# Ternary weights prepared in pieces during the last attention batch, with their sign test and load on GpSimd, and the first feed-forward steps spread over the attention's tail

## The chip, the cores and the metric

One core of one Trainium2 chip runs the whole program. The metric is the device time of one execution in microseconds (us), taken as the median of several runs.

## What is computed

Two transformer layers on x of 4 batches of 512 tokens, 256 wide. The first layer (windowed attention, then a mixture of experts) is untouched by the change. The second is full attention with 16 heads of width 16, then a feed-forward part whose two weight matrices (1024 by 256, and 256 by 1024) are replaced by ternary ones:

```
scale = maximum(mean(abs(w)), 1e-8)
w_q   = clip(round(w / scale), -1, 1)       # in the kernel: (w > scale/2) - (w < -scale/2)
h = gelu(x @ w1_q.T + b1);  out = h @ w2_q.T + b2
```

So the ternary weights need three passes over each matrix: a sum of absolute values (then a sum over the partitions, by a matmul with ones), a test against -scale/2, and a step that makes the test against +scale/2 and subtracts.

## The kernel before

The parts run one after the other: attention 0 (A), experts (B), attention 1 (C), feed-forward (D). Within C and D each engine runs its own program, written out by hand and tied to the others by semaphores.

**Part C.** `pair_step(b, n, new, old, following)` handles pair n (two heads, n = 0 to 7) of batch b, in eight places i = 0 to 7. At each place TensorE makes one score tile (L1689) into one of three PSUM banks, and VectorE takes its negated row maximum (L1006), which frees the bank: TensorE can be at most three tiles ahead. Older pairs are worked on at the same places: the transposed scores (L1702), their Exp on ScalarE (L1341), the products with the values (L1728), and every second pair a transpose (L1742), a reciprocal (L1033) and a scaling (L1035), after which the next transpose of the maxima (L1714) may use its bank. Extra work hangs on fixed places: the layer norm of the next batch (statistics in pair 1, L659), the projections of the next batch, the transposes of the previous batch's output (L1640) and its output projection (L1647). `keep_raw` (L1327) copies bank 0 to a two-slot ring `raw`, and GpSimd takes it from there: low parts (L600) or the residual add (L610). After the last batch, four more steps (`TAIL1 = 4`, `pair_step(BATCHES, n, False, True, False)`) finish what is under way, with no new score tiles.

**Part D.** `mlp_step(b, f, ...)` for f = 0 to 8: TensorE makes hidden tile f (L1837, four matmuls), ScalarE applies Gelu (L1393) and copies a high part (L1398), VectorE subtracts to get the low part (L1098), and TensorE multiplies tile f-2 by the second matrix (L1814, eight matmuls). At f = 8 the next batch is transposed (L1428). The steps of batch 0 stand after tail steps: `MLP_AFTER = {2: (0,), 3: (1, 2, 3, 4, 5, 6, 7, 8)}`, that is all but one behind the tail's last step.

**The ternary weights.** SyncE loads both matrices and a bias in batch 0 of C (L469, 1 MB each). VectorE takes the absolute sum of each whole matrix (L1071, 128x2048 elements) after pairs 6 and 7 of batch 0. In the tail, after step 0, TensorE sums over the partitions (L1849), and VectorE makes the scales (L1044 to L1048), then for each matrix a whole test (L1054, into `wneg`) and a whole `scalar_tensor_tensor` (L1056). TensorE waits for both before hidden tile 0.

GpSimd's order in the last batch of C: two low parts, the reciprocal root of the layer norm (L493), the norm's application (L593), two low parts, two residual adds; then the tail's two residual adds, and for each batch of D the bias (L639), with the reciprocal root of the next norm ahead of it.

Of the kernel before, what the change touches and what calls it, by code (L numbers as in the profile page):

```python
# [21 lines left out]
P = 128  # L22
BATCHES, SEQ, D = 4, 512, 256
TT = SEQ // P
KT = D // P
# [48 lines left out]
QUANT_EPS = 1e-8  # L74


def build(nc, dram, out):
    with ExitStack() as ctx:
# [92 lines left out]
        wabs = sb("wabs", [P, 2], where=part_c)  # L171
# [10 lines left out]
        sb("gap_c1", [P, 56], where=part_c)  # L182
# [16 lines left out]
        wneg = sb("wneg", [P, KT * DFF], where=part_d)  # L199
# [23 lines left out]
        wd_loaded, b2_loaded = sem("wd_loaded"), sem("b2_loaded")  # L223
# [125 lines left out]
        def _(sp):  # L349
# [132 lines left out]
        def _(pool):  # L482
# [128 lines left out]

            for b in range(BATCHES):
# [5 lines left out]
                norm_apply(i, (b + 1) % BATCHES)  # L618
                if b + 1 < BATCHES:
# [12 lines left out]
            for half in range(2):  # L632
                add_out(BATCHES, half, half)
# [10 lines left out]
            for b in range(1, BATCHES):  # L644
# [5 lines left out]
        def _(dve):  # L650
# [390 lines left out]
            def ternary_scales():  # L1041

                dve.wait_ge(wabs_summed, 1)
                V.tensor_scalar(wscl[:], ps[:, 1, 0:2], 1.0 / (DFF * D), QUANT_EPS, ALU.mult, ALU.max  # L1044
                                ).then_inc(quant_step, 1)
                dve.wait_ge(quant_step, 4)
                V.tensor_scalar(whalf[:], wscl[:], 0.5, None, ALU.mult).then_inc(quant_step, 1)
                V.tensor_scalar(wmhalf[:], wscl[:], -0.5, None, ALU.mult).then_inc(quant_step, 1)  # L1048
                dve.wait_ge(quant_step, 6)

            def ternary_weights(i):

                wait(dve, quantized, i)
                V.tensor_scalar(wneg[:], flat[i], wmhalf[:, i:i + 1], None, ALU.is_lt).then_inc(quant_step, 1)  # L1054
                dve.wait_ge(quant_step, 7 + i)
                V.scalar_tensor_tensor(tern[i], flat[i], whalf[:, i:i + 1], wneg[:], ALU.is_gt, ALU.subtract  # L1056
                                       ).then_inc(quantized, 1)
# [7 lines left out]
            for n in range(1, PAIRS):  # L1065
                pair_step(0, n, True, False, True)
                if n >= PAIRS - 2:

                    i = n - (PAIRS - 2)
                    dve.wait_ge(wd_loaded, 3 * 16)  # L1070
                    V.tensor_reduce(wabs[:, i:i + 1], flat[i], AX.X, ALU.add, apply_absolute_value=True  # L1071
                                    ).then_inc(quant_step, 1)
# [30 lines left out]
            for n in range(TAIL1):  # L1103
                pair_step(BATCHES, n, False, True, False)
                if n == 0:
                    ternary_scales()
                    ternary_weights(0)
                if n == 1:
                    ternary_weights(1)
                for f in MLP_AFTER.get(n, ()):  # L1110
                    mlp_step(0, f, True, False, True)
# [10 lines left out]
        def _(act):  # L1122
# [206 lines left out]
            def pair_step(b, n, new, old, following):  # L1329
# [604 lines left out]
```

## Time and profile before

| | us |
|---|---|
| median of 3 runs | 1415.06 (1414.72 to 1417.81) |
| the profiled execution, its own time | 1412.89 |
| its span in the profile | 1411.2 |
| TensorE busy | 1350.9 (96%) |
| VectorE busy | 1057.3 (75%) |
| ScalarE busy | 729.5 (52%) |
| GpSimd busy | 477.8 (34%) |
| mean granted TensorE clock | 0.977 of full speed |

The busy times are sums over parts with different limits. A row of the profile names the engine, the line, the tiles and the mean duration; PE is TensorE, PEld its weight loads, DVE VectorE, ACT ScalarE, POOL GpSimd and SP SyncE. A line of the timeline gives start and duration in us, then in brackets the idle time before it and what ended it. Part C runs from about 1056 to 1317, its four batches some 65 us each, the tail to about 1344, and D to the end at 1411.

### The profile page before, as it was taken

The page shows a single profiled execution, that of the slowest core. Times are in us where ns is not written, and L with a number is a line of the kernel's source. Part 1 is how long each engine was busy: PE and PEld are TensorE (multiplying, and loading weights), DVE is VectorE, ACT ScalarE, POOL GpSimd, SP SyncE. Part 2 cuts the span into 40 slices and gives each one's busy share as a digit, 9 for nine tenths or more (in the row PEclk, how much of TensorE's full clock was granted, in tenths as well). Part 3 has the DMA queues.
Part 4 walks back from the last instruction along what each step waited for, and adds up shares of the span by engine and source line. Part 5 has one row for each costly group of instructions (what it writes and reads, how often), then busy time and mean ns, then how long its engine had stood idle before and what let it go on. Part 6 is the DMA issues. An engine that isn't in the chain of part 4 may idle for free.

```text
span 1411.2 us, 25588 instructions
## 1 busy us (share of the span) xinstructions
PE 1350.9 (96%) x8082; PEld 1075.3 (76%) x8082; DVE 1057.3 (75%) x2464; ACT 729.5 (52%) x1899; POOL 477.8 (34%) x728
## 2 busy tenths in 40 slices
PE   5799999999999999899999999999999999999898
PEld 3688988988898899788888888888884344444487
DVE  6889999989999999567655455444647887787475
ACT  4775565556555655454432232233325676767465
POOL 5766657765776576200000000000003131321031
PEclk9999999999999999999999999999996999999899
DMA  5200000000000000045311211103152333332001
GB/s 183 86 30 1 2 1 2 2 4 1 1 2 1 1 1 1 24 150 157 125 46 60 62 38 61 65 30 102 61 179 104 105 105 121 113 127 76 0 16 45
DMA packets 45892, 80.92 MB, mean 57 GB/s; under 512 B 5608, under 2 KB 13928, under 8 KB 45484
## 3 DMA queue, kind: packets, MB, share of 16 engines
q1 hardware_dynamic: 45484, 79.35, 17.2%
q8 instruction: 60, 0.98, 0.3%
q14 instruction: 60, 0.49, 0.1%
q0 software_dynamic: 288, 0.10, 0.1%
HBM read 64.70 MB, written 15.87 MB: 57 GB/s over the span
## 4 chain that ended last, share of the span: by engine, by line
PE 68%; DVE 13%; issue 5%; POOL 3%; ACT 2%; DVEq 0%; ACTq 0%; POOLq 0%
PE ps L1419 14%; PE ps L1421 13%; PE ps L1420 13%; PE ps L1689 5%; PE ps L1728 5%; PE ps L1506 3%; PE ps L1462 3%; PE ps L1814 2%; DVE ssum L805 2%; DVE qkn L794 2%; PE ps L1837 2%; DVE yT L769 1%; PE ps L1714 1%; PE ps L1702 1%; DVE nmax L785 1%
## 5 line engine op out<-in xcount | busy, mean ns | idle before, releaser
L1006 DVE TENSOR_REDUCE nm<-ps 128x1 f32<-128x512 f32 x256 | 166.1, 684 | 51.8 <-PE ps L1689 51.5
L1341 ACT ACTIVATE pT<-ps 128x512 f32<-128x512 f32 x256 | 143.5, 598 | 65.2 <-PE ps L1702 63.2
L493 POOL TENSOR_TENSOR ln_rs<-ln_ve,minus_half 128x4 f32<-128x4 f32 x12 | 15.1, 1262 | 434.0 <-DVE ln_ve L666 434.0
L1419 PE MATMUL ps<-xnT_lo,w1moe_hi 128*128 128x512 f32 x400 | 160.2, 401 | 0.0
L1420 PE MATMUL ps<-xnT_hi,w1moe_lo 128*128 128x512 f32 x400 | 159.0, 397 | 0.0
L1421 PE MATMUL ps<-xnT_hi,w1moe_hi 128*128 128x512 f32 x400 | 158.9, 397 | 0.0
L918 DVE TENSOR_TENSOR sg<-ps,sg 128x512 f32<-128x512 f32 x100 | 69.0, 690 | 116.8 <-ACT sg L1269 116.5
L1252 ACT ACTIVATE moe_act_hi<-sg 128x512 fp32r<-128x512 f32 x100 | 63.2, 632 | 149.6 <-DVE sg L930 149.6
L1419 PE MATMUL ps<-wqkv_lo,xnT_hi 128*128 128x512 f32 x256 | 127.4, 498 | 6.7 <-DVE xnT_lo L708 2.8
L534 POOL TENSOR_TENSOR rope<-rope 128x384 f32<-128x384 f32 x128 | 132.7, 1037 | 0.0
L1269 ACT ACTIVATE sg<-ps 128x512 f32<-128x512 f32 x100 | 59.6, 596 | 128.3 <-PE ps L1421 121.5
L1506 PE MATMUL ps<-qkT 128*128 128x128 f32 x896 | 121.4, 276 | 0.0
L1419 PE MATMUL ps<-w2moe_lo,moe_act_hi 128*128 128x256 f32 x400 | 114.1, 285 | 5.9 <-DVE moe_act_lo L936 5.9
L936 DVE TENSOR_TENSOR moe_act_lo<-sg,moe_act_hi 128x512 fp32r<-128x512 f32 x100 | 69.1, 691 | 62.4 <-ACT moe_act_hi L1252 62.4
L1702 PE MATMUL ps<-qsm,kst 64*128 64x512 f32 x256 | 111.9, 491 | 3.2 <-ACT pT L1341 3.0
L532 POOL TENSOR_TENSOR rms<-msq,minus_half 128x3 f32<-128x3 f32 x128 | 110.6, 864 | 10.0
L1421 PE MATMUL ps<-w2moe_hi,moe_act_hi 128*128 128x256 f32 x400 | 112.3, 281 | 0.0
L1420 PE MATMUL ps<-w2moe_hi,moe_act_lo 128*128 128x256 f32 x400 | 112.0, 280 | 0.0
L1506 PEld LDWEIGHTS ps<-qkT 128*128 128x128 f32 x896 | 110.6, 192 | 0.5
L1689 PE MATMUL ps<-kst,qst 64*128 64x512 f32 x256 | 105.0, 482 | 4.3 <-DVE nm L1006 3.7
L1161 ACT ACTIVATE probT<-ps 128x256 f32<-128x256 f32 x128 | 49.4, 386 | 112.5 <-PE ps L1462 56.5
L1209 ACT ACTIVATE yT<-ps,nmax 128x128 f32<-128x128 f32 x256 | 92.6, 375 | 26.4 <-DVE nmax L785 26.2
(203 smaller groups left out, 3762.7 us busy)
## 6 DMA issues: line engine op xcount, KB each, us to landing
c_rows<-comb_rows SPq DMA_DIRECT2D x36, 256.0 KB, 3.2
copies<-qk_hi SPq DMA_DIRECT2D x32, 256.0 KB
qst<-copies SPq DMA_DIRECT2D x32, 256.0 KB, 2.6
kst<-copies SPq DMA_DIRECT2D x32, 256.0 KB, 2.9
yT<-in_w1moe SPq DMA_DIRECT2D x25, 256.0 KB, 2.6
x_res<-in_wqkv SPq DMA_DIRECT2D x8, 512.0 KB, 4.7
copies<-qk_lo SPq DMA_DIRECT2D x16, 256.0 KB
c_rows<-comb_rows SPq DMA_DIRECT2D x16, 224.0 KB, 3.0
```

The lines of the kernel that those rows point to most:

```text
L532: nc.gpsimd.tensor_tensor(rms[:, s, :], msq[:, s, :], minus_half[:, 0:3], ALU.pow).then_inc(rms_ready, 1)
L534: nc.gpsimd.tensor_tensor(rope1[:, s, :], rope1[:, s, :], rope2[:, s, :], ALU.add).then_inc(rotated, 1)
L1006: V.tensor_reduce(nm1[:, n % 2, t, col:col + 1], ps[:, 1 + s1_slot(p), :], AX.X, ALU.max, negate=True).then_inc(s1_max, 1)
L1209: ins = A(prob[:, m % PROB_RING, h, :], ps[:, 3 + s, (2 * h + 1) * P:(2 * h + 2) * P], ACT.Exp, bias=nmax[:, s, h:h + 1], accum_out=psums[ ...
L1341: A(pT1[:, u % 2, 2 * (m % 2) + h, c, :], ps[:, 4 + e % 2, :], ACT.Exp, scale=SCALE1).then_inc(p1_ready, 1)
L1419: MM(out, left[0], right[1], start=first, stop=False, skip_group_check=True)
L1420: MM(out, left[1], right[0], start=False, stop=False, skip_group_check=True)
L1421: return MM(out, left[0], right[0], start=False, stop=last, skip_group_check=True)
L1506: ins = MM(bank[:, h, part, :], qkT[:, m % K_RING, h, :], qkT[:, (m if part else m - GROUPS) % K_RING, 2, :], start=not alone(m) and h == ...
L1689: MM(ps[:, 1 + s1_slot(p), :], qst[rows, n % STACK_RING, t * P:(t + 1) * P], kst[rows, n % STACK_RING, :], start=True, stop=True).then_inc ...
L1702: MM(ps[:, 4 + e % 2, :], kst[rows, m % STACK_RING, c * P:(c + 1) * P], qsm[rows, m % 2, :], start=True, stop=True).then_inc(st_ready, 1)
L1728: ins = MM(ps[VW * h:VW * (h + 1), 6, :], v1[:, c, col:col + VW], pT1[:, u % 2, h, c, :], start=c == 0, stop=c == TT - 1, tile_position=(0 ...
```

## The change

1. The three loads move from SyncE to GpSimd's queue, one in each of batches 0, 1 and 2, behind the batch's bias add.
2. The two whole sums in batch 0 become eight sums of 128x512 in pairs 0 to 3 of the last batch, at places 2 and 6. The sum over the partitions comes at place 5 of pair 4, into bank 0, and the scales behind place 6.
3. The test against -scale/2 moves to GpSimd: four pieces of 128x1024, ahead of its last two residual adds of the batch. `wneg` becomes twice as large.
4. The two whole `scalar_tensor_tensor` become eight of 128x512 on VectorE, at places 1, 3 and 5 of pairs 5 and 6 and places 1 and 3 of pair 7. Each waits for GpSimd's piece.
5. The steps 0 to 8 of batch 0 of D are spread over the four tail steps, by place. The first product with the second matrix waits for the last Exp, since they share two banks.
6. GpSimd makes the first bias add and the reciprocal root for batch 1's norm ahead of the tail's residual adds.

```diff
+WABS_PARTS, TERN_PARTS, SIGN_PARTS = 4, 4, 2
...
-        MLP_AFTER = {2: (0,), 3: (1, 2, 3, 4, 5, 6, 7, 8)}
+        MLP_AFTER = {(0, 3): 0, (0, 7): 1, (1, 6): 2, (2, 1): 3, (2, 4): 4, (2, 6): 5, (3, 0): 6, (3, 2): 7, (3, 7): 8}
+        SCALES_AT = (4, 5)
+        SUM_AT = {(n, i): 2 * n + i // 4 for n in range(4) for i in (2, 6)}
+        TERN_AT = {(5 + q // 3, 1 + 2 * (q % 3)): q for q in range(2 * TERN_PARTS)}
...
-                    if b == 0 and n == PAIRS_T + 1:
-                        sp.wait_ge(gu_ready, BATCHES * FT)
-                        for name, dst in (("wm1", wm1), ("wm2", wm2), ("b1m", b1m)):
-                            sp.dma_start(dst[:], dram[name]).then_inc(wd_loaded, 16)
...
+            def sign_weights():
+
+                pool.wait_ge(quant_step, 2 * WABS_PARTS + 5)
+                for q in range(2 * SIGN_PARTS):
+                    i, at = q // SIGN_PARTS, slice(q % SIGN_PARTS * (KT * DFF // SIGN_PARTS),
+                                                   (q % SIGN_PARTS + 1) * (KT * DFF // SIGN_PARTS))
+                    nc.gpsimd.tensor_scalar(wneg[:, i, at], (wm1, wm2)[i][:].rearrange("p a f -> p (a f)")[:, at],
+                                            wmhalf[:, i:i + 1], None, ALU.is_lt).then_inc(below_ready, 1)
...
                     add_bias(b + 1)
+                    name, dst = (("wm1", wm1), ("wm2", wm2), ("b1m", b1m))[b]
+                    pool.dma_start(dst[:], dram[name]).then_inc(wd_loaded, 16)
...
+                if b == BATCHES - 1:
+                    sign_weights()
...
-            for half in range(2):
-                add_out(BATCHES, half, half)
...
             add_bias2(0)
-            for b in range(1, BATCHES):
+            rstd(2 * BATCHES + 1)
+            for half in range(2):
+                add_out(BATCHES, half, half)
+            add_bias2(1)
+            for b in range(2, BATCHES):
...
+            def weight_sums(q):
+
+                i, wide = q // WABS_PARTS, KT * DFF // WABS_PARTS
+                V.tensor_reduce(wabs[:, q:q + 1], flat[i][:, q % WABS_PARTS * wide:(q % WABS_PARTS + 1) * wide],
+                                AX.X, ALU.add, apply_absolute_value=True).then_inc(quant_step, 1)
+
+            def ternary_weights(q):
+
+                i, wide = q // TERN_PARTS, KT * DFF // TERN_PARTS
+                at = slice(q % TERN_PARTS * wide, (q % TERN_PARTS + 1) * wide)
+                dve.wait_ge(below_ready, q * SIGN_PARTS // TERN_PARTS + 1)
+                V.scalar_tensor_tensor(tern[i][:, at], flat[i][:, at], whalf[:, i:i + 1], wneg[:, i, at],
+                                       ALU.is_gt, ALU.subtract).then_inc(quantized, 1)
...
+            dve.wait_ge(wd_loaded, 3 * 16)
             for n in range(PAIRS):
-                pair_step(BATCHES - 1, n, True, True, False)
+                for i in range(2 * TT):
+                    pair_step(BATCHES - 1, n, True, True, False, (i,))
+                    if (n, i) in SUM_AT:
+                        weight_sums(SUM_AT[n, i])
+                    if (n, i) == (SCALES_AT[0], SCALES_AT[1] + 1):
+                        ternary_scales()
+                    if (n, i) in TERN_AT:
+                        if TERN_AT[n, i] == 0:
+                            for tile in range(2):
+                                dve.wait_ge(copies_kept[tile], KEPT_COPIES * BATCHES)
+                        ternary_weights(TERN_AT[n, i])
...
+                    if not old and m == 0:
+                        pe.wait_ge(p1_ready, BATCHES * PAIRS * 2 * TT)
...
             for n in range(TAIL1):
-                pair_step(BATCHES, n, False, True, False)
...
+                for i in range(2 * TT):
+                    pair_step(BATCHES, n, False, True, False, (i,))
+                    if (n, i) in MLP_AFTER:
+                        if MLP_AFTER[n, i] == 0:
+                            pe.wait_ge(quantized, 2 * TERN_PARTS)
+                        mlp_step(0, MLP_AFTER[n, i], True, False, True)
```

## Rows read from the trace of the kernel before

**Rows 1.** Busy time by stretch: start:end, length, busy time (x instructions), PEclk, DMA
```profile
1190.00:1253.00 63.00, 61.91 (x376) 30.29 (x378) 48.79 (x90) 44.71 (x85) 18.56 (x14) 1.00 0.34 114
1317.00:1344.00 27.00, 22.82 (x97) 12.46 (x96) 11.36 (x13) 13.26 (x22) 4.55 (x3) 0.81 0.00 1
```

**Rows 2.** Timeline of PE, ends of batches 0 and 1
```profile
1110.65 0.63 PE L1714 MATMUL ps<-ident,nm 128*128 128x128 f32 x4 [0.28 <-DVE otok L1035]
...
1113.35 0.49 PE L1689 MATMUL ps<-kst,qst 64*128 64x512 f32 x1 [1.64 <-DVE nm L1006]
...
1129.48 0.63 PE L1714 MATMUL ps<-ident,nm 128*128 128x128 f32 x4 [0.28 <-DVE otok L1035]
...
1178.58 0.63 PE L1714 MATMUL ps<-ident,nm 128*128 128x128 f32 x4 [0.27 <-DVE otok L1035]
...
1179.80 1.99 PE L1647 MATMUL ps<-wo,oTn 128*128 128x256 f32 x8
...
1194.28 0.63 PE L1714 MATMUL ps<-ident,nm 128*128 128x128 f32 x4 [0.27 <-DVE otok L1035]
```

**Rows 3.** Groups of DVE by form, from 900 on: busy us, mean ns
```profile
L1056 DVE SCALAR_TENSOR_TENSOR wt<-wm,whalf,wneg 128x2048 fp32r<-128x2048 f32 x2 | 4.7, 2350 | 0.1
L1071 DVE TENSOR_REDUCE wabs<-wm 128x1 f32<-128x2048 f32 x2 | 4.6, 2276 | 0.0
```

**Rows 4.** Timeline of DVE in the last batch: pairs 1, 2 and 5
```profile
1262.50 1.27 DVE L1006 TENSOR_REDUCE nm<-ps 128x1 f32<-128x512 f32 x2
1263.69 0.42 DVE L659 BATCH_NORM_STATS2 bn_st<-x_res 128x6 f32<-128x256 f32 x1
1264.07 1.29 DVE L1006 TENSOR_REDUCE nm<-ps 128x1 f32<-128x512 f32 x2
...
1272.23 0.69 DVE L1006 TENSOR_REDUCE nm<-ps 128x1 f32<-128x512 f32 x1 [0.98 <-PE ps L1689]
...
1292.22 0.68 DVE L1015 TENSOR_TENSOR qsm<-ps,qst 128x512 fp32r<-128x512 f32 x1
1292.82 2.47 DVE L1006 TENSOR_REDUCE nm<-ps 128x1 f32<-128x512 f32 x4
1295.52 1.29 DVE L1006 TENSOR_REDUCE nm<-ps 128x1 f32<-128x512 f32 x2 [0.23 <-PE ps L1689]
```

**Rows 5.** Waits in 1250 to 1316: total us, times, longest
```profile
DVE nm L1006 <- PE ps L1689: 12.7, 26, 1.3
```

**Rows 6.** Groups of POOL by form: busy us, mean ns
```profile
L593 POOL TENSOR_SCALAR xn<-x_res,bn_mv,ln_rs 128x256 f32<-128x256 f32 x16 | 19.4, 1225 | 0.7 <-POOL ln_rs L493 0.7
L573 POOL TENSOR_TENSOR x_res<-x_res,bo 128x1024 f32<-128x1024 f32 x4 | 9.5, 2385 | 21.3 <-DVE x_res L901 21.0
L518 POOL TENSOR_SCALAR_AFFINE_SELECT parted<-probT 128x256 f32<-128x256 f32 x96 | 41.8, 435 | 18.4 <-ACT probT L1161 18.1
L487 POOL DMA_DIRECT2D causal<-in_c_causal x1 | 0.5, 546 | 0.0
```

**Rows 7.** Timeline of DVE and POOL side by side, batch 0 of D
```profile
1341.98 2.38 POOL L639 TENSOR_TENSOR x_res<-x_res,b2r 128x1024 f32<-128x1024 f32 x1
...
1342.37 2.55 DVE L1098 TENSOR_TENSOR hact_lo<-hact,hact_hi 128x512 fp32r<-128x512 f32 x1 [9.87 <-ACT hact_hi L1398]
```

**Rows 8.** Timeline of ACT in the tail
```profile
1317.03 0.60 ACT L1341 ACTIVATE pT<-ps 128x512 f32<-128x512 f32 x1 [0.57 <-PE ps L1702]
...
1321.51 1.30 ACT L1341 ACTIVATE pT<-ps 128x512 f32<-128x512 f32 x2 [0.18 <-PE ps L1702]
1328.15 0.60 ACT L1373 ACTIVATE oT<-ps 128x512 f32<-128x512 f32 x1 [5.34 <-PE ps L1728]
1328.77 1.28 ACT L1393 ACT_TABLE_LOAD   x1
1330.43 0.69 ACT L1393 ACTIVATE hact<-ps,b1m 128x512 f32<-128x512 f32 x1 [0.38 <-PE ps L1837]
1331.15 0.63 ACT L1398 ACTIVATE hact_hi<-hact 128x512 fp32r<-128x512 f32 x1
```

**Rows 9.** Chain that ended last: start, us, what; tail and after
```profile
1333.66 3.68 PE ps L1647 x8
1337.37 0.61 ACT raw L1327
1338.02 1.99 PE ps L1647 x8
...
1349.65 0.95 PE ps L1814 x8
1350.60 0.94 PE ps L1837 x4
...
1354.44 0.87 PE ps L1428 x8
```

**Rows 10.** Busy time by stretch, as rows 1, in the tail
```profile
1320.00:1322.00 2.00, 2.00 (x3) 0.76 (x3) 1.93 (x3) 1.69 (x3) 0.00 (x0) 0.50 0.00 0
1334.00:1336.00 2.00, 2.00 (x6) 1.55 (x6) 0.00 (x0) 0.00 (x0) 0.00 (x0) 0.50 0.00 0
```

More of the change, by code:

```diff
@@ L170, in build @@
         b1m = sb("b1m", [P, HT], where=part_c)
-        wabs = sb("wabs", [P, 2], where=part_c)
+        wabs = sb("wabs", [P, 2 * WABS_PARTS], where=part_c)
+        wsum = sb("wsum", [P, 2], where=part_c)
         wscl = sb("wscl", [P, 2], where=part_c)
@@ L181, in build @@
         ones = sb("ones", [P, P], where=part_c)
-        sb("gap_c1", [P, 56], where=part_c)
+        sb("gap_c1", [P, 48], where=part_c)
         qk1 = [sb(f"qk1_{part}", [P, 2, 2, SEQ], F32R, part_c) for part in ("hi", "lo")]
@@ L198, in build @@
         part_d = ExitStack()
-        wneg = sb("wneg", [P, KT * DFF], where=part_d)
+        wneg = sb("wneg", [P, 2, KT * DFF], where=part_d)
         part_d.close()
@@ L618, in _ @@
                 norm_apply(i, (b + 1) % BATCHES)
+                if b == 0:
+                    pool.wait_ge(gu_ready, BATCHES * FT)
                 if b + 1 < BATCHES:
@@ L1066, in _ @@
                 pair_step(0, n, True, False, True)
[L1067 to L1072, printed above, removed]
             with dve.Fori(1, BATCHES - 1) as b:
@@ L1327, in keep_raw, with pair_step @@
                 A(raw[:, off % 2, :], ps[:, 0, :], ACT.Copy).then_inc(raw_kept, 1)
-            def pair_step(b, n, new, old, following):
+            def pair_step(b, n, new, old, following, places=range(2 * TT)):
                 kb, kq = b * PAIRS, b * (PAIRS // 2)
                 valid = lambda m: new if m >= 0 else old
-                for i in range(2 * TT):
+                for i in places:
                     m = n - 1 if i >= TT else n - 2
@@ L1402, in _ @@
             for n in range(TAIL1):
-                pair_step(BATCHES, n, False, True, False)
-                for f in MLP_AFTER.get(n, ()):
-                    mlp_step(0, f, True, False, True)
+                for i in range(2 * TT):
+                    pair_step(BATCHES, n, False, True, False, (i,))
+                    if (n, i) in MLP_AFTER:
+                        mlp_step(0, MLP_AFTER[n, i], True, False, True)
             with act.Fori(1, BATCHES - 1) as b:
@@ L1782, in pair_step @@
                             pe.wait_ge(raw_kept, before + (6 if following else 4))
+                            if not following:
+                                pe.wait_ge(quant_step, 2 * WABS_PARTS + 2)
                         pe.wait_ge(oTn_ready, KT * b)
@@ L1803, in _ @@
             for n in range(PAIRS):
-                pair_step(BATCHES - 1, n, True, True, False)
+                for i in range(2 * TT):
+                    pair_step(BATCHES - 1, n, True, True, False, (i,))
+                    if (n, i) == SCALES_AT:
+                        pe.wait_ge(quant_step, 2 * WABS_PARTS + 1)
+                        pe.wait_ge(raw_kept, raw_before(BATCHES - 1) + 4)
+                        MM(ps[:, 0, 0:2 * WABS_PARTS], ones[:], wabs[:], start=True, stop=True).then_inc(wabs_summed, 1)
             def mlp_step(b, f, new, old, following):
                 def down(m):
+                    if not old and m == 0:
+                        pe.wait_ge(p1_ready, BATCHES * PAIRS * 2 * TT)
                     pe.wait_ge(h_split, b * HT + m + 1)
@@ L1843, in _ @@
             for n in range(TAIL1):
[L1844 to L1853 removed]
+                for i in range(2 * TT):
+                    pair_step(BATCHES, n, False, True, False, (i,))
+                    if (n, i) in MLP_AFTER:
+                        if MLP_AFTER[n, i] == 0:
+                            pe.wait_ge(quantized, 2 * TERN_PARTS)
+                        mlp_step(0, MLP_AFTER[n, i], True, False, True)
             with pe.Fori(1, BATCHES - 1) as b:
```

33 lines of the change are left out of this document (7 added, 26 removed).

## The prediction

> **What bounds the kernel now.** I read the busy time by stretch first. In a middle batch of attention 1 TensorE is busy 61.9 of 63 us and VectorE 48.8 [rows 1], so a batch goes by TensorE, with VectorE not far behind. The tail is different: 27 us in which VectorE is busy 11.4, ScalarE 13.3 and the clock averages 0.81. Nothing fills it; one dependent step follows another. Next come the waits: in the last batch VectorE waited 12.7 us in all, 26 times, at most 1.3 at once, for the next score tile [rows 5]. That is all the room there is for new VectorE work. Last comes the chain through the tail [rows 9].
>
> The profiled execution took 1412.89 against a span of 1411.2, and lies 2.2 under the median of the runs shown, 1415.06. I work out a difference on its trace and add it to the median. About 0.2% (2.8 us) is what a measurement of this kernel can tell from no change.
>
> **1. Batch 0 loses its two whole sums.** The stretch from the maxima's transpose in pair 7 to that in pair 1 of the next batch takes 1129.48 - 1110.65 = 18.83. The same stretch one batch on takes 1194.28 - 1178.58 = 15.70, and holds an output projection of some 1.92 (1.99 with its pipelined end) that batch 0 hasn't got: 13.78 [rows 2]. The sums cost 5.05 there, though their own time is 4.55 [rows 3], since TensorE stood for 1.64 [rows 2] and lost its clock behind it. I take -5.0. The bounds are -3.0, should the projection's places be hidden work, and -5.0.
>
> **2. The loads.** They leave SyncE, whose stacks were not waited for. On GpSimd an issue costs 0.55 [rows 6], at a place with nothing due behind it for several us. I take 0, and 1 us if a load delays a stack.
>
> **3. Eight sums in the last batch.** A quarter of 2276 ns is 0.57 [rows 3], and a 128x512 reduction starts the next 0.60 later (1263.69 - 1262.50 is 1.19 for two [rows 4]). That makes 4.8 us. In pairs 0, 2 and 3 VectorE has gaps (one of 0.98 [rows 4]) and two places to be late by, so I charge 0.3, 0.5 and 0.5. In pair 1, with the norm's statistics, it has no gap at all [rows 4], and both pieces count nearly in full: 1.0. Sum +2.3. The scales are four small dependent operations: +0.5. Bounds: 0 if the gaps take everything, +5.4 if they take nothing.
>
> **4. The ternary pieces, and who holds whom.** A piece of `scalar_tensor_tensor` is a quarter of 2350 plus a start, 0.65 [rows 3]; eight are 5.2. But it has two SBUF operands while GpSimd reads SBUF. The trace shows what that does: a 128x512 subtraction with two SBUF operands, 0.69 elsewhere, took 2.55 us because GpSimd's add ran from 1341.98 to 1344.36; it ended 0.56 behind it [rows 7]. The reductions, with one operand in PSUM, show nothing of the kind.
> The Trainium skill, page "SBUF — State Buffer", section "Who interferes with whom", says that a VectorE instruction with two SBUF inputs contends with a GpSimd instruction that reads SBUF, the later one blocked fully; by that rule each early piece waits out a whole GpSimd piece, and the trace agrees (2.55 us); without it this part would be 4.1 cheaper.
> What is GpSimd's piece of 128x1024? No row shows it. The tensor_scalar with two operations takes 1225 ns for 256 elements, so at most 4.9 us for 1024; the affine select takes 435 ns for 256, so 1.7; an add over 1024 takes 2.4 [rows 6]. Half of the first (one operation instead of two) is 2.45 and meets the add. I take 2.4 and keep 1.7 and 4.9.
> The scales end near 1290.0 (old clock of the trace; the delays of part 3 shift everything alike). GpSimd's pieces: 1290.0 to 1292.4, the second to 1294.8. VectorE comes to its first piece at 1293.1, with maxima addition and scaling behind it [rows 4], and is held to 1294.8, ends 1295.5. GpSimd's third piece runs to 1297.9; after two reductions VectorE asks at 1296.7, and ends 1298.5. The fourth runs to 1300.9; VectorE asks at 1299.7 and ends 1301.5. Before, it had finished this place at 1295.3: late by 6.2, of which 4.1 is being held. TensorE can be three tiles ahead and takes up about one; but standing still costs it its clock, as in part 1, so I let the two cancel. The five later pieces meet a free port and gaps: +0.6. Sum +6.8. Bounds: +2.7 without any holding; with pieces of 4.9 us, laid out the same way, the third ternary piece ends at 1311.6 instead of 1301.5, so +16.9.
>
> **5. The tail.** Work of TensorE that is there in any case: Exp's source tiles, 32 value products (4.0 at full clock), two transposes, 3.84 of projection, and steps of 0.95 + 0.94 [rows 9]. From 1316.5 to the next batch's transpose at 1354.44 [rows 9] are 37.9; the work, at full clock, is about 27. So 11 us could go. What stands against it is ScalarE. Hidden tiles 0 and 1 now stand among the last Exps, at (0,3) and (0,7). Gelu needs another table than Exp: one load of 1.28 [rows 8] becomes five. Eight Exps lay between 1317.03 and 1322.8 [rows 8]; with four more loads (5.1) and two Gelu-and-copy pairs (2.5, 1330.43 to about 1331.7 for one [rows 8]), less what idle time takes up, they end near 1329.1. The value products need them, so they begin at 1328.4 instead of 1322.1. From there: 4.0 + six steps of 1.9 + 0.66 + 1.2 + 3.84 = 21.1, and waits of 3.2 (1.8 where the scaling at (2,7) stands behind tile 5's subtraction on VectorE, 0.7 twice for a raw copy as at 1337.37 [rows 9]). The transpose comes at 1352.7, a gain of 1.7. The clock is down where ScalarE paces [rows 10], and a low clock at the start of the products takes some 0.7 back: -1.0. Bounds: -8 (loads hidden), +3 (a second low-clock stretch, worth the 1.75 that one projection lost there before: 3.68 against 1.92 [rows 9]).
> The Trainium skill, "ScalarE: Activation LUTs", "What ACT_TABLE_LOAD costs", gives about 2.66 us for a switch with its drain; by that figure the four extra switches would be 10.6 instead of 5.1 and the tail would lose; no row here shows the drain.
> The old whole tests and ternary passes in the tail are costed at nothing: they ended at 1327.5, under 5.96 us of value products that ran to 1328. Tests on GpSimd delay its residual adds, which nothing waits for that soon. The earlier bias add no longer holds the subtraction in batch 0 of D [rows 7]; that is in the tail's count.
>
> **Sum.** -5.0 + 2.3 + 0.5 + 6.8 - 1.0 = +3.6. 1415.06 + 3.6 = 1418.7.
>
> **The rivals.**
> (a) *GpSimd's test is slow.* With a start of some 0.2 counted once, four times 1225 ns come to 4.3 us a piece; laid out as above the third ternary piece ends 7.7 later: 1426.4 (1428.8 at 4.9). For it: the only tensor_scalar on GpSimd costs 4.8 ns an element. Against: two operations there. It decides above some 3.3 us a piece. 0.20.
> (b) *The tail really fills*, and the kernel is faster. If the table loads fall into ScalarE's waits for score tiles, the Exps end three to four us earlier and the steps cover the transposes: -8 instead of -1. Then 1411.7, and less with short tests. It decides from a tail gain of 7.5. For it: 37.9 us against 27 of work. Against: five loads in a row of Exps that ScalarE already paces. 0.25.
> (c) *Little or no holding*: pieces of 1.7 us hold for about 0.6 each, part 4 costs 4.3 and the time is 1416.2; with no holding at all it costs 2.7: 1414.6. The 2.55 us row [rows 7] speaks against it. 0.15.
> The forecast itself has 0.40, and runs from 1415 to 1422.
>
> **The numbers.** Faster by over 0.2% is (b), 0.25. Within 0.2% (1412.2 to 1417.9) are (c), 0.15, and the low quarter of the forecast, 0.10. Slower: the rest of the forecast, 0.30, and (a), 0.20. Faster and slower cases both matter, so the range reaches from 1409 (most of (b)) to 1427 (most of (a)).
>
> **What would show it.** Batch 0's end 5 us shorter, with no clock dip near 1115. The last batch 9 to 10 us longer. Rows of `scalar_tensor_tensor` of 128x512 with two or three far above 0.65, each ending about 0.6 behind a GpSimd test; the test's row near 2.4. Five table loads in the tail where there was one, the last Exp some 6 us later relative to the batch's end. I am wrong if the pieces all take 0.65, if the tests take 4 us or more, if the last batch grows by under 5, or if the tail from the last score tile to batch 1's transpose shrinks by more than 5.

## The result, and the profile after

The changed kernel took 1417.37 us, the kernel before 1415.67 beside it (20 runs each). The ratio is 1.0017, with a 95% interval from 1.0009 to 1.0025: slower by 2.4 us (1.3 to 3.5; the medians themselves lie 1.7 apart). The interval lies clear of 1, but most of it is under the 0.2% that I had taken for the least that a measurement can tell. The forecast was 1418.7 in a range of 1409 to 1427. The time lies in the range, on the side of "slower" but within the 0.2% that I called "same" and gave 0.25. It came about in another way than the one I had worked out, so the stretches are what to read.

The profiled execution has a span of 1417.0 (1411.2 before), 5.8 more. The maxima's transpose in place 1 of a pair is a mark that stands in both kernels. These are marks of the changed kernel in TensorE's timeline: the end of batch 0 (the mark of pair 7, then that of pair 1 of the next batch), which answers to [rows 2], and those of pairs 5 and 6 of the last batch with what stood between them. The marks of pair 7 and of the tail follow at 1308.12 and 1315.63.

```profile
1113.06 0.63 PE L1745 MATMUL ps<-ident,nm 128*128 128x128 f32 x4 [0.28 <-DVE otok L1055]
...
1127.76 0.63 PE L1745 MATMUL ps<-ident,nm 128*128 128x128 f32 x4 [0.28 <-DVE otok L1055]
...
1290.23 0.63 PE L1745 MATMUL ps<-ident,nm 128*128 128x128 f32 x4 [0.45 <-DVE otok L1055]
...
1293.98 0.50 PE L1720 MATMUL ps<-kst,qst 64*128 64x512 f32 x1 [1.41 <-DVE nm L1026]
...
1299.28 0.66 PE L1745 MATMUL ps<-ident,nm 128*128 128x128 f32 x4
```

From mark to mark, in us, with the same marks of the kernel before:

| stretch | before | after | difference | predicted |
|---|---|---|---|---|
| up to pair 7 of batch 0 | 1110.65 | 1113.06 | +2.4 | 0 |
| batch 0 pair 7 to batch 1 pair 1 | 18.83 | 14.70 | -4.1 | -5.0 |
| from there to pair 0 of the last batch | 121.07 | 121.08 | 0 | 0 |
| last batch, pairs 0 to 4 (the sums) | 33.18 | 33.69 | +0.5 | +2.3 |
| last batch, pair 4 to 5 (the scales) | 7.53 | 7.70 | +0.2 | +0.5 |
| pair 5 to 6 (three ternary pieces) | 6.05 | 9.05 | +3.0 | +6.2 |
| pair 6 to 7, pair 7 to the tail (five pieces) | 15.96 | 16.35 | +0.4 | +0.6 |
| tail, up to batch 1's transpose of xn | 41.01 | 44.34 | +3.3 | -1.0 |
| from there to the end | 56.92 | 57.03 | +0.1 | 0 |

The 2.4 us ahead of pair 7 of batch 0 are scatter between single executions: at the mark of pair 0 of batch 0, ahead of everything that was changed, the two traces are already 2.6 apart (1063.06 and 1065.62). The stretches behind pair 7's mark sum to +3.4 in the trace, against +3.6 predicted and +2.4 measured. The agreement of the sum is luck: the tail is 4.3 worse than predicted, the ternary pieces 3.4 and the sums 2.1 better.

The groups of instructions of the new work, by form (busy us, mean ns), which answer to [rows 3] and [rows 6]:

```profile
L621 POOL TENSOR_SCALAR wneg<-wm,wmhalf 128x1024 f32<-128x1024 f32 x4 | 11.8, 2967 | 4.2 <-DVE wmhalf L1071 4.2
L1085 DVE SCALAR_TENSOR_TENSOR wt<-wm,whalf,wneg 128x512 fp32r<-128x512 f32 x8 | 6.7, 836 | 0.0
L1077 DVE TENSOR_REDUCE wabs<-wm 128x1 f32<-128x512 f32 x8 | 5.4, 675 | 0.0
...
L637 POOL DMA_DIRECT2D wm<-in_wm x2 | 1.3, 664 | 0.0
```

The test of 128x1024 on GpSimd, for which no row stood before, takes 2.97 on average where I took 2.4. A sum takes 0.675. The mean of the eight ternary pieces, 0.836, hides one that is twice as long as the others. The timelines of the two engines side by side (answering to [rows 4] and [rows 7]) show it:

```profile
1288.84 2.85 POOL L621 TENSOR_SCALAR wneg<-wm,wmhalf 128x1024 f32<-128x1024 f32 x1 [4.17 <-DVE wmhalf L1071]
1291.67 2.84 POOL L621 TENSOR_SCALAR wneg<-wm,wmhalf 128x1024 f32<-128x1024 f32 x1
1294.49 3.35 POOL L621 TENSOR_SCALAR wneg<-wm,wmhalf 128x1024 f32<-128x1024 f32 x1
```

```profile
1291.84 1.49 DVE L1085 SCALAR_TENSOR_TENSOR wt<-wm,whalf,wneg 128x512 fp32r<-128x512 f32 x1
1293.25 1.27 DVE L1026 TENSOR_REDUCE nm<-ps 128x1 f32<-128x512 f32 x2
1294.44 0.76 DVE L1085 SCALAR_TENSOR_TENSOR wt<-wm,whalf,wneg 128x512 fp32r<-128x512 f32 x1
...
1296.33 0.73 DVE L1085 SCALAR_TENSOR_TENSOR wt<-wm,whalf,wneg 128x512 fp32r<-128x512 f32 x1
```

In the gaps between the lines VectorE did maxima. The first piece began 0.17 behind a test and took 1.49, 0.75 too long, but ended 1.2 ahead of the test's end. The second and third ran wholly beside a test in 0.76 and 0.73. VectorE waited out no instruction of GpSimd. Yet it works without a gap here up to 1298.3, and the pair takes 3.0 longer on TensorE, 1.41 of it as a stand ahead of 1293.98 in the fence before.

Between 1250 and 1316 VectorE now waits less for score tiles (5.7 us in 12 waits, against the 12.7 of [rows 5]): of the 12.1 us of new work, some 7 went into waits.

```profile
DVE nm L1026 <- PE ps L1720: 5.7, 12, 0.9
```

The tail in ScalarE's timeline, answering to [rows 8]:

```profile
1318.84 1.28 ACT L1423 ACT_TABLE_LOAD   x1
1320.14 0.69 ACT L1423 ACTIVATE hact<-ps,b1m 128x512 f32<-128x512 f32 x1
...
1321.51 1.28 ACT L1371 ACT_TABLE_LOAD   x1
...
1326.66 1.28 ACT L1423 ACT_TABLE_LOAD   x1
...
1329.42 1.28 ACT L1371 ACT_TABLE_LOAD   x1
...
1332.19 1.09 ACT L1371 ACTIVATE pT<-ps 128x512 f32<-128x512 f32 x2 [0.39 <-PE ps L1733]
1333.29 1.28 ACT L1423 ACT_TABLE_LOAD   x1
```

Five table loads, as predicted, and ScalarE's last Exp ends at 1333.28, 17.65 behind the tail's mark (before it was 9.5: 1322.8 against 1313.27). TensorE's own timeline shows what stood still because of it:

```profile
1323.45 0.79 PE L1733 MATMUL ps<-qsm,kst 64*128 64x512 f32 x1 [2.73 <-ACT pT L1371]
...
1331.36 1.28 PE L1733 MATMUL ps<-qsm,kst 64*128 64x512 f32 x2 [2.20 <-ACT pT L1371]
...
1348.45 0.66 PE L1671 MATMUL ps<-ident,otok 128*128 128x128 f32 x4 [1.84 <-DVE otok L1055]
...
1357.29 1.99 PE L1678 MATMUL ps<-wo,oTn 128*128 128x256 f32 x8 [0.69 <-ACT raw L1357]
```

Busy time by stretch, where PEclk is the third column from the end, answers to [rows 1] and [rows 10]:

```profile
1292.00:1301.00 9.00, 7.49 (x41) 2.23 (x43) 8.11 (x13) 3.81 (x7) 8.65 (x3) 0.81 0.22 75
1322.00:1336.00 14.00, 10.35 (x26) 4.99 (x27) 3.45 (x14) 10.80 (x15) 1.04 (x1) 0.51 0.00 1
1317.00:1344.00 27.00, 22.07 (x101) 11.47 (x98) 6.62 (x21) 18.85 (x26) 1.04 (x1) 0.75 0.00 1
```

The projections of [rows 9] take 1.74 and 2.01 in the chain of the changed kernel, where the first had taken 3.68: the low clock has left them, and has gone elsewhere. Two stretches lost theirs. In pair 5 the mean is 0.81. In the tail it is 0.51 for 14 us, nearly all of it at the lower of the two levels (1.2 GHz); ScalarE was busy for 10.8 of them, and TensorE waited in between.

### The profile page after: what moved, and what is told of

The parts are those of the page before. It is cut to its first block, busy times and chain, and to the rows that moved or that the text cites. A ratio compares the mean times of both kernels' runs of the same rounds, so it can differ in the third digit from the quotient of the medians.

```text
span 1417.0 us, 25612 instructions
## 1 busy us (share of the span) xinstructions
PE 1352.5 (95%) x8082; PEld 1077.2 (76%) x8082; DVE 1052.7 (74%) x2475; ACT 734.3 (52%) x1903; POOL 490.5 (35%) x735
## 4 chain that ended last, share of the span: by engine, by line
PE 66%; DVE 15%; issue 5%; POOL 3%; ACT 3%; DVEq 0%; DMA 0%; SPq 0%; ACTq 0%; POOLq 0%
PE ps L1450 13%; PE ps L1452 13%; PE ps L1451 13%; PE ps L1720 5%; PE ps L1759 4%; PE ps L1537 3%; PE ps L1493 3%; PE ps L1855 2%; DVE ssum L825 2%; PE ps L1878 2%; DVE qkn L814 2%; DVE yT L789 1%; DVE nmax L805 1%; PE ps L1745 1%; DVE nm L1026 1%
```

## The experiments

Four questions were open. Is it the tail that loses, and through the table loads? What do the whole sums of batch 0 cost? Is pair 5 late through GpSimd, or through VectorE's own work? What holds a VectorE instruction, and for how long? Each ratio is to the kernel before, measured beside it on the same chip. e1 to e4 share one chip, e5 to e7 another, and e8 stands on a third, so their ratios are compared and not their times. A length of a stretch comes from one traced execution each.

**The first steps of D back behind the tail (e1).**

```
-        MLP_AFTER = {(0, 3): 0, (0, 7): 1, (1, 6): 2, ..., (3, 7): 8}
+        MLP_PE = MLP_ACT = MLP_DVE = {(2, 7): (0,), (3, 7): (1, 2, 3, 4, 5, 6, 7, 8)}
```

> The kernel after the change, with the steps of batch 0 of D put back behind tail steps 2 and 3, so that only the parts ahead of the tail are new. After the change the stretch from the maxima's transpose at place 1 of tail step 0 to batch 1's transpose grew from 41.0 to 44.3 us. Theory T (the new tail is what loses): the stretch is back at 41 or a little less, since the ternary passes no longer stand in it, and the whole is about 3.3 us shorter than after the change, level with the kernel before (ratio 0.999 to 1.001). Rival R (the tail is longer because of what comes ahead of it, a VectorE or GpSimd late from the last batch): the stretch stays near 44 and the time does not move.

Ratio 1.0001 (0.9988 to 1.0014), 1413.85 us, span 1412.6. The marks of the tail in TensorE's timeline:

```profile
1315.56 0.65 PE L1747 MATMUL ps<-ident,nm 128*128 128x128 f32 x4
...
1355.71 1.03 PE L1461 MATMUL ps<-ident,xn 128*128 128x128 f32 x8
```

The tail takes 40.15 instead of 44.34, and 0.9 less than before the change (41.01), when whole tests and ternary passes stood in it; 0.9 is within what two executions of one tail can differ by (see e4). So without the spreading, moving the weights' preparation out of the tail would have broken even; the spreading loses. By the ratios (1.0017 against 1.0001) it loses 2.3 us, give or take 2.2, and not the 4.2 of the two traces.

**Gelu behind the last Exp (e2).** TensorE's places stay as changed. ScalarE and VectorE do their steps 0 and 1 at place (1, 3), behind the last Exp.

```
-        MLP_AFTER = {(0, 3): 0, (0, 7): 1, (1, 6): 2, ...}
+        MLP_PE = {(0, 3): (0,), (0, 7): (1,), (1, 6): (2,), ...}
+        MLP_ACT = MLP_DVE = {(1, 3): (0, 1), (1, 6): (2,), ...}
```

> The kernel after the change, with TensorE's places as they are, but on ScalarE and VectorE the steps of hidden tiles 0 and 1 moved behind the last Exp (tail step 1, place 3). One table load in the tail instead of five. Theory T (the table loads between Exps hold the value products): the last Exp ends near 10 us after the place-1 transpose instead of 17.7, the value products start 7 to 8 us sooner, and the stretch to batch 1's transpose falls from 44.3 to 37 to 39; the whole is 5 to 7 us shorter than after the change, 0.997 to 0.998 of before. Rival R (the spreading itself costs: steps in front of the value products and one engine's order behind another's): the stretch stays at 43 or more.

Ratio 0.9985 (0.9975 to 0.9995), 1411.78 us, span 1410.5. The tail takes 37.82. ScalarE's timeline:

```profile
1324.46 2.27 ACT L1373 ACTIVATE pT<-ps 128x512 f32<-128x512 f32 x4 [0.96 <-PE ps L1735]
1326.75 1.28 ACT L1425 ACT_TABLE_LOAD   x1
1328.04 0.69 ACT L1425 ACTIVATE hact<-ps,b1m 128x512 f32<-128x512 f32 x1
```

One load is left, and the last Exp ends 11.0 behind the mark instead of 17.65. So the spreading is worth 2.3 us against e1's tail as far as TensorE goes (40.15 to 37.82), and what turned that into a loss were two tiles of Gelu among the Exps, with their four extra loads (no run moved the loads alone). Against the changed kernel the ratios give 4.5 us, where I expected 5 to 7 and the two spans differ by 6.5.

**The tests on VectorE (e3).** Each ternary piece is preceded by its own test on VectorE, and GpSimd does none.

```
-                dve.wait_ge(below_ready, q * SIGN_PARTS // TERN_PARTS + 1)
+                V.tensor_scalar(wneg[:, i, at], flat[i][:, at], wmhalf[:, i:i + 1], None, ALU.is_lt
+                                ).then_inc(below_ready, 1)
+                dve.wait_ge(below_ready, q + 1)
```

> The kernel after the change, with the test against -scale/2 made by VectorE in front of each ternary piece (128x512, fast mode, some 0.35 us each) and none on GpSimd. Pair 5 of the last batch (transpose to transpose) took 6.05 before and 9.05 after. Theory T1 (pair 5 is bound by VectorE, which had no gap there, and pays for all VectorE work in it, 2.2 us of pieces): with three more tests pair 5 takes 6.05 + 3 x 0.66 + 3 x 0.35 = 9.1 plus what the low clock adds, so 9 to 10, no shorter than after the change. Rival R1 (the contention with GpSimd is what pair 5 pays for): the first piece no longer takes 1.49, nothing waits for GpSimd, and pair 5 falls to 7.5 or less.

Ratio 1.0062 (1.0046 to 1.0078), 1421.62 us. Pair 5 to 6 took 8.98, as in the changed kernel, although GpSimd did nothing beside it. Three tests of 0.48 on VectorE, 1.5 us with their starts, replaced the hold of 0.75 and the wait of 0.89 for a score tile with which VectorE ended the pair in the changed kernel. It is the lower end of my 9 to 10, and far from the 7.5 of the rival. Pair 6 to 7 took 10.57 (8.84 after) and pair 7 to the tail 9.75 (7.51). One piece was held here too, by something else. One line of VectorE's timeline, then one of GpSimd's:

```profile
1310.92 1.65 DVE L1075 SCALAR_TENSOR_TENSOR wt<-wm,whalf,wneg 128x512 fp32r<-128x512 f32 x1
```

```profile
1310.70 1.32 POOL L613 TENSOR_TENSOR x_res<-raw,x_res 128x512 f32<-128x512 f32 x1 [21.27 <-ACT raw L1347]
```

It took 1.65 beside GpSimd's residual add, and ended 0.55 behind the add's end. So the tests belong on GpSimd, which saves 4 us over pairs 6 and 7 in these traces. By the ratios it saves 0.45%, 6.4 us in all.

**The whole sums back in batch 0 (e4).** Two sums of 128x2048 stand at the ends of pairs 6 and 7 of batch 0, with SyncE loading the weights; the rest is as changed.

```
-        WABS_PARTS, TERN_PARTS, SIGN_PARTS = 4, 4, 2
+        WABS_PARTS, TERN_PARTS, SIGN_PARTS = 1, 4, 2
-        SUM_AT = {(n, i): 2 * n + i // 4 for n in range(4) for i in (2, 6)}
+        SUM_AT = {}
...
                 pair_step(0, n, True, False, True)
+                if n >= PAIRS - 2:
+                    dve.wait_ge(wd_loaded, 3 * 16)
+                    weight_sums(n - (PAIRS - 2))
```

> The kernel after the change, with the two whole sums and SyncE's three loads back in batch 0; everything else stays. From the maxima's transpose in pair 7 of batch 0 to that in pair 1 of batch 1 took 18.83 before and 14.70 after. Theory T (the whole sums stop TensorE and take its clock; in pieces they are hidden in gaps): the stretch is back at 18 to 19, pairs 0 and 1 of the last batch lose the 0.2 and 0.35 us that the pieces cost, and the whole is 3 to 4 us longer than after the change (ratio to before 1.004). Rival R (the loads on SyncE caused the loss in batch 0): impossible to tell in this run from the sums, but then the low clock would start before the first whole sum. If neither matters the stretch stays at 14.7.

Ratio 1.0041 (1.0026 to 1.0056), 1420.05 us. The marks of pair 7 of batch 0 and pair 1 of the next:

```profile
1117.09 0.63 PE L1750 MATMUL ps<-ident,nm 128*128 128x128 f32 x4 [0.29 <-DVE otok L1057]
...
1135.95 0.63 PE L1750 MATMUL ps<-ident,nm 128*128 128x128 f32 x4 [0.28 <-DVE otok L1057]
```

18.86, as before the change (18.83). The loads went back together with the sums, so this run alone doesn't part the two; but the granted clock is 1.00 up to the stand of 1.64 behind the first sum (which begins at 1116.86) and 0.50 only from 1122 on, which speaks for the sums. By the ratios the pieces save 0.24% (give or take 0.17), 3.4 us, which fits the 4.1 of this stretch less the half us that the pieces cost later. This run told something else as well. Its tail, with the very instructions of the changed kernel, took 42.01 against 44.34 (marks at 1323.32 and 1365.33), with nearly the same stands of TensorE (2.73, 2.41 and 1.85 against 2.73, 2.20 and 1.84). What differs is the granted clock: 0.63 over the 14 us that begin 6.4 behind the tail's mark, where the changed kernel had 0.51, and 1.00 instead of 0.71 in the 4 us from the end of the stand of 1.84.

```profile
1329.70:1343.70 14.00, 10.16 (x32) 5.24 (x33) 3.43 (x14) 11.32 (x16) 1.04 (x1) 0.63 0.00 1
```

So single executions of this tail differ by 2.3 us with nothing but the clock to tell them apart, and its loss against the one trace of before is +1.0 to +3.3. The lower of the two fits the ratios of e1 and e2 better.

**The pieces out of pair 5 (e5).** On top of e2.

```
-        TERN_AT = {(5 + q // 3, 1 + 2 * (q % 3)): q for q in range(2 * TERN_PARTS)}
+        TERN_AT = {(6, 1): (0,), (6, 3): (1,), (6, 5): (2,), (7, 1): (3,), (7, 3): (4,), (7, 5): (5,), (7, 7): (6, 7)}
```

> As the kernel with the two Gelu steps behind the last Exp, and the eight ternary pieces of VectorE stand in pairs 6 and 7 alone (6,1), (6,3), (6,5), (7,1), (7,3), (7,5), (7,7) twice, none in pair 5. GpSimd's four tests stand where they stood. In the changed kernel pair 5 to 6 took 9.05 us (before 6.05), 6 to 7 8.84 (before 8.83), pair 7 to the tail 7.51 (before 7.13). Theory V (pair 5 has no slack on VectorE: 8 x 0.6 us of its own work fill its 6.05 us, while pairs 6 and 7 have some): pair 5 to 6 goes back to 6.1 to 6.4, pairs 6 and 7 become longer by 1 us at most in all, and the span is 2 to 3 us below the kernel with the two Gelu steps late (1410.5), about 1408; its profiled time 0.15 to 0.2% better. Rival G (pair 5 is late because GpSimd's tests disturb VectorE, wherever VectorE's pieces stand): pair 5 to 6 stays above 8 us. Rival S (the eight pieces cost their 6 us wherever they stand): what pair 5 gains, pairs 6 and 7 lose, and the span stays at 1410.5.

Ratio 0.9986 (0.9972 to 1.0000), 1412.96 us, span 1410.4: nothing gained against e2. The marks of pairs 5 and 6 and of the tail (pair 7's is at 1304.66):

```profile
1289.76 0.63 PE L1747 MATMUL ps<-ident,nm 128*128 128x128 f32 x4 [0.45 <-DVE otok L1057]
...
1295.81 0.66 PE L1747 MATMUL ps<-ident,nm 128*128 128x128 f32 x4
...
1314.12 0.66 PE L1747 MATMUL ps<-ident,nm 128*128 128x128 f32 x4 [1.89 <-DVE nm L1028]
```

Pair 5 to 6 is back at 6.05, exactly as before the change, with GpSimd's tests still beside it. That settles pair 5: it paid for VectorE's three pieces, of which one was held, and not for GpSimd's tests as such (theory V against G). Pair 6 took its three pieces for nothing (8.85). But pair 7 to the tail grew from 7.51 to 9.46, with a stand of 1.89, and the tail from 37.82 to 39.29. My expectation of 1408 was wrong, and the traces of the next two kernels show through what.

**The scaling ahead of tile 5 (e6).** On top of e5, VectorE's step 5 moves from (2, 6) to (2, 7), behind the scaling of the output rows.

```
-        MLP_DVE = {..., (2, 4): (4,), (2, 6): (5,), (3, 0): (6,), ...}
+        MLP_DVE = {..., (2, 4): (4,), (2, 7): (5,), (3, 0): (6,), ...}
```

> The kernel before this one, and VectorE's low part of hidden tile 5 stands one place later, (2,7) for (2,6), behind the scaling of the output rows (otok) that TensorE waits 1.8 us for at place (2,7). Theory O (that wait is VectorE's order: it does the subtraction of tile 5, and waits for ScalarE's high part of it, ahead of the scaling): the wait of 1.8 us is gone and the tail 1.3 to 1.8 us shorter than in the kernel without the move. Rival (the scaling waits for the products of the last heads anyway): the wait stays within 0.3 us of 1.8, and so does the tail.

Ratio 0.9977 (0.9964 to 0.9990), 1412.43 us, span 1409.5. The wait of 1.8 is gone and the tail takes 37.31, 2.0 less than in e5 (theory O). The intervals of e5 and e6 overlap widely, so only the traces tell these two apart. VectorE's timeline in pair 7, and GpSimd's:

```profile
1309.19 0.74 DVE L1087 SCALAR_TENSOR_TENSOR wt<-wm,whalf,wneg 128x512 fp32r<-128x512 f32 x1
...
1311.05 2.92 DVE L1087 SCALAR_TENSOR_TENSOR wt<-wm,whalf,wneg 128x512 fp32r<-128x512 f32 x1
```

```profile
1311.05 2.37 POOL L657 TENSOR_TENSOR x_res<-x_res,b2r 128x1024 f32<-128x1024 f32 x1
```

The piece that I had moved to (7, 5) met GpSimd's addition of the bias, whose two operands are both in SBUF, and took 2.92 instead of 0.74, 0.55 beyond that addition. In the changed kernel this addition (1313.40 to 1315.78) stands beside reductions from PSUM only, and they are hardly longer for it (2.56 for four, 2.47 in [rows 4]).

**The two engines by themselves (e7, one execution).** Behind the last output step of the changed kernel VectorE does 40 pieces of 128x512; GpSimd does four tests, four subtractions with two SBUF operands, and last two tests alone.

```
+            for k in range(40):          # VectorE
...
+                V.scalar_tensor_tensor(hact2[0][:, k % 3, :], flat[0][:, at], whalf[:, 0:1], hact[:, 0, :],
+                                       ALU.is_gt, ALU.subtract).then_inc(trial_dve, 1)
...
+            for k in range(10):          # GpSimd
...
+                    nc.gpsimd.tensor_scalar(wt2[...][:, at], w, wmhalf[:, 1:2], None, ALU.is_lt)
+                    nc.gpsimd.tensor_tensor(wt2[...][:, at], w, w, ALU.subtract)
```

> The changed kernel, and behind its last output step VectorE does 40 scalar_tensor_tensor of 128x512 (two operands in SBUF): 4 alone, 16 from the moment that GpSimd begins 4 tests of 128x1024 (one operand in SBUF), 20 from the moment that GpSimd begins 4 subtractions of 128x1024 with two operands in SBUF; last, GpSimd does 2 tests alone. (Theory 1, no holding by tests: VectorE's pieces take 0.74 us beside the tests as alone, but for one or so of 1.5 at a start; GpSimd's tests 2.85 beside VectorE and alone. Theory 2, my prediction's: each test holds the VectorE instruction that comes up to it until it ends, so pieces of over 2 us stand beside the tests, one for each.) Beside subtractions both theories have VectorE held, 1 us or more for some pieces: the 128x512 subtraction of VectorE took 2.55 us beside one of GpSimd's before, where it takes 0.6 alone.

Timelines of the two engines, from the tests on (the second fence is GpSimd's; its last line is a test alone):

```profile
1424.40 1.52 DVE L1171 SCALAR_TENSOR_TENSOR hact_hi<-wm,whalf,hact 128x512 fp32r<-128x512 f32 x1
...
1431.27 2.38 DVE L1171 SCALAR_TENSOR_TENSOR hact_hi<-wm,whalf,hact 128x512 fp32r<-128x512 f32 x1
...
1441.79 0.74 DVE L1171 SCALAR_TENSOR_TENSOR hact_hi<-wm,whalf,hact 128x512 fp32r<-128x512 f32 x1
```

```profile
1423.65 3.45 POOL L678 TENSOR_SCALAR wt<-wm,wmhalf 128x1024 fp32r<-128x1024 f32 x1
...
1430.78 2.32 POOL L680 TENSOR_TENSOR wt<-wm 128x1024 fp32r<-128x1024 f32 x1 [0.25 <-DVE spare L1167]
1433.06 2.33 POOL L680 TENSOR_TENSOR wt<-wm 128x1024 fp32r<-128x1024 f32 x1
...
1450.70 2.84 POOL L678 TENSOR_SCALAR wt<-wm,wmhalf 128x1024 fp32r<-128x1024 f32 x1 [10.71 <-DVE spare L1175]
```

Beside tests, one piece for each test is held, near the test's start, and takes 1.52 to 1.61; the others take 0.74 as alone. The test pays too where a piece is running as it begins: 3.27 to 3.45 instead of 2.84. The changed kernel shows the two apart: the test behind which the held piece began took 2.84, and the next, 0.05 behind the start of a piece that wasn't held, took 3.35. Beside subtractions VectorE gets exactly one piece done for each of GpSimd's instructions, 2.38 each, ending 0.55 behind it, and GpSimd isn't slowed (2.33). This is what my theory expected of tests: it holds for GpSimd's instructions with two SBUF operands and not for those with one.

**Three pieces out of pair 7 (e8).** On top of e6, the last three pieces stand in the tail, where VectorE had 6.4 us of nothing; TensorE's first up-projection waits for the first matrix alone. No piece stands beside the whole of that addition any more.

```
+        TERN_AT = {(6, 1): (0,), (6, 3): (1,), (6, 5): (2,), (7, 1): (3,), (7, 3): (4,)}
...
                     pair_step(BATCHES, n, False, True, False, (i,))
+                    if (n, i) == (0, 0):
+                        for q in range(5, 2 * TERN_PARTS):
+                            ternary_weights(q)
...
-                        if f == 0:
-                            pe.wait_ge(quantized, 2 * TERN_PARTS)
+                        if f < 2:
+                            pe.wait_ge(quantized, (f + 1) * TERN_PARTS)
```

> The kernel with the tile-5 step behind the scaling, and five of VectorE's ternary pieces in pairs 6 and 7 (6,1), (6,3), (6,5), (7,1), (7,3), the last three in the tail's place (0,0), where VectorE stood idle for 6.4 us; TensorE's first up-projection waits for the first matrix alone, the second for both. Theory H (what the late pieces cost in pair 7 was one piece held for 2.92 us beside GpSimd's addition of two operands in SBUF, 128x1024, 2.37 us; beside the tests a piece is held once, by 0.8): with no piece beside that addition pair 7 to the tail goes from 9.45 back to 7.2 to 7.6, no piece takes over 1.7, and the span goes from 1409.5 to 1407 to 1408. Rival S (eight pieces cost about what they take, wherever they stand, in the tail too): the span stays within 0.5 us of 1409.5, and the tail gets longer by what pair 7 gives back.

Ratio 0.9934 (0.9917 to 0.9951), 1406.32 us beside 1415.27, span 1404.4. It beats the kernel before by 0.66%, and by the ratios the changed one too. VectorE's and TensorE's timelines around the tail:

```profile
1310.81 2.98 DVE L1087 SCALAR_TENSOR_TENSOR wt<-wm,whalf,wneg 128x512 fp32r<-128x512 f32 x3
...
1318.48 0.26 DVE L1055 RECIPROCAL oinv<-ps 128x16 f32<-128x16 f32 x1 [4.10 <-PE ps L1778]
```

```profile
1311.75 0.66 PE L1750 MATMUL ps<-ident,nm 128*128 128x128 f32 x4
...
1347.44 1.09 PE L1464 MATMUL ps<-ident,xn 128*128 128x128 f32 x8 [0.69 <-ACT raw L1362]
```

Pair 7 to the tail is back at 7.51 (theory H). The three moved pieces take 2.98, the first of them 0.9 of holding by the end of the same addition (1309.53 to 1311.91), and VectorE still has 4.1 us of nothing behind them. The tail takes 35.69, 1.6 less than in e6; expected was that pair 7's 1.9 would be the gain, and the span came out 2.6 under the lower end of the expectation; 1.5 of that lie ahead of pair 7 (its mark at 1304.24, in e6 at 1305.77), in parts that are the same. What the tail gained I did not take apart by a run of its own, nor what the shorter wait of TensorE for the ternary weights gives. The traces place it, though: the last Exp ends 12.55 behind the tail's mark in e6 and 10.98 in e8, which is all of the 1.6. e6's tail begins behind the stand of 1.88, e8's doesn't, and this is the busy time of the first 4 us of each:

```profile
1315.22:1319.22 4.00, 4.00 (x20) 1.28 (x22) 1.87 (x3) 1.09 (x2) 0.00 (x0) 0.64 0.00 0
1311.75:1315.75 4.00, 4.00 (x26) 1.70 (x26) 2.63 (x4) 2.10 (x4) 0.16 (x1) 1.00 0.00 0
```

TensorE is busy throughout in both, at a clock of 0.64 in e6 and 1.00 in e8. e5, with a stand of 1.89, has 0.59 and 12.54, and e2, with none, 1.00 and 10.99. So the late pieces of pair 7, the held one above all, were paid for twice, as 1.9 in their pair and as 1.6 at a low clock behind it. Together these undid the 3.0 that e5 had gained in pair 5.

## Why the prediction came out as it did

**Step 1, the whole sums: right in kind, too large.** -4.1 where I took -5.0, inside my bounds, and e4 brings the stretch back to 18.86. The estimate compared batch 0 with a batch whose projection I subtracted at its full 1.92; the 0.9 us between would be what of the projection other work hides (no run tested that). The clock dip is gone: before, it was 0.50 from 1116 to 1118, and after the change it is 1.00 from 1108 to 1128.

**Step 2, the loads: right.** An issue costs 0.66 on GpSimd, and nothing was due behind it.

**Step 3, eight sums: a term mis-sized.** They cost +0.5, not +2.3 (scales +0.2, not +0.5). I charged pair 1 with 1.0 because VectorE had no gap there; it grew by 0.35 (7.12 to 7.47). Pair 0 grew by 0.17, and in pairs 2 and 3 nothing was added (9.28 both; 8.26 to 8.25). That VectorE's waits of 12.7 us are "all the room there is" was too strict: a place may also be late by the tiles that TensorE is ahead. I had counted two such places for pairs 0, 2 and 3, and none for pair 1.

**Step 4, "held to the end of GpSimd's piece": the step that failed.** I carried over the 2.55 of [rows 7], a subtraction beside an *addition*, to tests, which read one SBUF operand. In the trace one piece was held by 0.75 and the other two of pair 5 not at all, and e7 reproduces both kinds in isolation. The 4.1 us that I charged for being held were 0.75. The length of the test was also off (2.84 alone, not 2.4), but without the whole hold that hardly counts, and rival (a), which lived on both, had nothing to stand on. Rival (c), with little holding, described the mechanism: it priced part 4 at +2.7 to +4.3, and it came to +3.4.
Of the +3.0 in pair 5, 3 x 0.66 is VectorE's own work in a pair where it had been busy for 5.46 of 6.05 us, 0.75 the hold; the 0.3 that remain may be the clock's (0.81), which no run tested. Moving the pieces one pair on made it 6.05 again (e5).
The Trainium skill, page "SBUF — State Buffer", section "Who interferes with whom", has a VectorE instruction with two SBUF inputs contend with any GpSimd instruction that reads SBUF, calls the port pair that they share an exclusive lock, and writes of the later one as fully blocked where VectorE runs in a two-port mode. I read all of it as one rule. For tests this case does not agree with that (0.74 beside a running test, one of 1.5 to 1.6 for each test in e7); for additions and subtractions with two SBUF operands it does (2.38 beside 2.33).

**Step 5, the tail: wrong sign, by single traces.** Predicted -1.0; +3.3 in this trace, +1.0 in that of e4. The mechanism that I named was the right one: five loads, Exps late, a wait of 1.8 for the scaling, twice 0.7 for a raw copy; all of them are there. Two sizes failed. In the times of the old trace (2.36 earlier) the last Exp ends at 1330.9 and the value products begin at 1330.2, where I had 1329.1 and 1328.4, since ScalarE also had to wait for score tiles (1.17 and 0.39) that TensorE could not make while it stood. And from there to batch 1's transpose it took 27.4 instead of 24.3. I had allowed 0.7 for the clock; it was 0.51 for 14 us, fell again behind the wait of 1.84, and the difference in clock from e4, which lost some too (0.63), is worth 2.3 by itself. e2 shows the tail without the loads: 37.82, a gain of 3.2 against before, so rival (b)'s filling exists in part, and the two Gelu steps with their loads take it all.

**The sum.** Errors of -2.1, -3.4 and +4.3, with +0.9 of step 1, cancelled to within 0.3 of the +3.6. The time was in the range by luck: of the five parts two came about as I had them. One of my own signs of being wrong was met as well: the last batch, from the mark of pair 0 to that of the tail, grew by 4.1 (62.72 to 66.79), where I had said 9 to 10 and "wrong" under 5. Of the signs of being right, one piece and not two or three was far above 0.65, and it ended 1.2 ahead of a test's end instead of 0.6 behind it; and the last Exp came 8.1 later relative to the batch's end, not some 6. The one chance that I should have set otherwise is that of no or little holding: 0.15, with a row about a different kind of instruction as the only argument against it.

## What to carry to other kernels

Work that is moved into gaps costs what the least idle pair of the engine leaves, not its share of all gaps: put pieces where the engine waits, and look at what GpSimd runs in those very microseconds, since here a piece with two SBUF operands cost its own time beside a one-operand instruction, and at most 0.9 more once, but lasted until half a microsecond behind the end of a two-operand one. When steps with another ScalarE function are interleaved to fill TensorE, let TensorE's part go early and keep ScalarE's part behind the last use of the old table. A stand of TensorE of 1.6 to 2.7 us was paid for a second time at half the clock in most traces here, and not in all (the stands of 1.85 in e2, e4 and e5).

## What was not expected of the hardware

- A GpSimd test of 128x1024 with one SBUF operand holds a VectorE instruction with two for 0.3 to 0.9 us, at most once for each test and near its start. In the changed kernel, in e6 and in all four tests of e7 the hold ended at the same point, 0.92 behind the test's start, if the start is taken as 2.84 ahead of its end (an estimate from the durations). A test that begins while such a piece runs is itself lengthened, from 2.84 to between 3.27 and 3.45. A subtraction with two SBUF operands (2.33) holds it to the end and half a microsecond more (2.38 a piece), without being slowed.
- GpSimd's tensor_scalar of 128x1024 with one operation takes 2.84 us, longer than an addition of two tensors of that size (2.33 to 2.38).
- The same instructions in the tail took 42.01 and 44.34 us in two executions, with nearly equal waits and a granted clock of 0.63 and 0.51 over 14 us.
- A table load and the start of the activation behind it took 1.30 (1318.84 to 1320.14, and 1321.51 to 1322.80 in the same tail); the 1.39 behind the load at 1326.66 was a wait for TensorE's tile, which ended at 1328.01. No row here shows the drain. The Trainium skill, "ScalarE: Activation LUTs", section "What ACT_TABLE_LOAD costs", gives twice that for a switch with its drain; by that figure, as an estimate, the four extra loads alone would be 10.6 us.
